# A small language-model tower in one kernel: another order of steps, sums and norms in its mixer

## The chip, the cores and the metric

The kernel runs as one program on one core of a Trainium2 chip. The metric is the device time of one execution in microseconds (us); lower is better. A core has a matrix engine (TensorE, PE in the profile), three engines for element-wise work (VectorE = DVE, ScalarE = ACT, GpSimd = POOL) and SyncE (SP), which issues most DMAs. Each engine works through its own queue in order, and semaphores tie the queues together.

## The reference

16 sequences of 128 tokens (2048 rows of width 192, 16 tiles of 128 rows) go through an embedding with a LayerNorm, an attention block, a mixer and a mixture of experts, all in float32:

```python
h = _L0_tok_ref(ids, types, token_emb, pos_emb, type_emb, gamma, beta)
h = h + attn(layernorm(h))                 # 8 heads of 192, softmax, projection
h = h + ffn(layernorm(h))                  # the function below

def ffn(x):
    h = _ln(x, ln1_g, ln1_b)               # a second norm of the normed rows
    q, k, v = split(h @ in_w.T + in_b)     # 12 heads of 16
    attn = softmax(q @ k.T / 4)            # over the 128 tokens of a sequence
    x = x + (attn @ v) @ out_w.T + out_b
    x = x + gelu(x @ mlp_w1 + mlp_b1) @ mlp_w2 + mlp_b2
    xm = _ln(x, ln2_g, ln2_b)
    return x + sum over the top 2 of 4 experts of gate * (gelu(xm @ w1 + b1) @ w2 + b2)
```

The mixer of the kernel is the part of `ffn` up to and with the line with `out_w`. Its input x is a normed row, so it needs two norms of each row, the norm and the norm of the norm.

## The kernel before, in words

Four stages follow each other, with all engines meeting in between: `embed`, `attention` (8 turns of 2 tiles), `mixer` (line 750, 16 tiles in 4 units of 4), and `experts`.

In attention each engine walks the same text of steps (`TURN`, line 353); words with a + are work for the next turn and are left out of the last. Ahead of the last turn SyncE asks for 14 finished tiles of h1 for the mixer (line 485).

In the mixer a list `order` (lines 799 to 828) names steps, and each engine walks it (`walk_order`), doing its own part of each step. The steps are: N, norms of a unit, in 15 parts, on VectorE; X, 8 transposes of the normed rows and their split into a high and a low half (ScalarE, then VectorE); Q0 to Q2, projections of q and k, of five passes each; V0 to V3, of v; S, the scores of a tile (12 heads in 4 strips of 3) and their row maxima on VectorE; M, the exponentials on ScalarE, 12 of 128x128; T, 12 transposes of them on TensorE, copied out strip by strip by ScalarE; A, the mix with v and, with a matrix of ones, the sums of the probabilities (lines 986, 990), which VectorE inverts as 128x384 numbers and multiplies in (lines 1138, 1141) to make the context; O, the projection out (line 999), which VectorE adds to the rows (line 1147) and SyncE stores.

For tile t the order is S(t), T(t-1), M(t), A(t-1), parts of the next unit's X, Q, V and N, O(t-1). TensorE writes X, Q, V, T, A and O into four banks in turn (`ring`); a slot waits until the slot four before it has been emptied (`emptied`, line 858). The scores have four banks of their own and are written when the exponentials before them have been read.

Beside this GpSimd prepares the weights of the experts: for each of 5 it loads them, splits off the high halves with three one-operand instructions (lines 908 to 910) and makes the low halves with three two-operand ones (lines 911 to 913). In the mixer the short helper lines 123 to 144 are those of moments and inverse roots.

## Time and profile before

| what | value |
|---|---|
| time, median of 3 runs | 1055.23 us (1053.48 to 1067.02) |
| the profiled execution's own time | 1057.01 us |
| its span, first to last instruction | 1055.3 us |
| TensorE busy | 824.1 us (78%) |
| VectorE, ScalarE, GpSimd busy | 545.9, 466.9, 229.9 us |

The page cuts the span into 40 slices of 26.4 us; a digit is the busy share in tenths, PEclk the granted clock of TensorE in tenths of full speed. The mixer lies in slices 18 to 27 (of 1 to 40).

```profile
PE   0039999999999999953365658655499999999997
DVE  5944242424334342327967775441456655765664
...
POOL 6221120202020111216761000000241250260260
PEclk9999999999999999985688988786699999999999
```

In a timeline row the first number is the start in us from the span's beginning, the second the length; then come engine, line, operation, what is written and read, and how many instructions are merged. In square brackets stands how long the engine was idle before, and what released it.

### The profile page before, as it was taken

The page shows a single profiled execution, that of the slowest core. Times are in us where ns is not written, and L with a number is a line of the kernel's source. Part 1 is how long each engine was busy: PE and PEld are TensorE (multiplying, and loading weights), DVE is VectorE, ACT ScalarE, POOL GpSimd, SP SyncE. Part 2 cuts the span into 40 slices and gives each one's busy share as a digit, 9 for nine tenths or more (in the row PEclk, how much of TensorE's full clock was granted, in tenths as well). Part 3 has the DMA queues.
Part 4 walks back from the last instruction along what each step waited for, and adds up shares of the span by engine and source line. Part 5 has one row for each costly group of instructions (what it writes and reads, how often), then busy time and mean ns, then how long its engine had stood idle before and what let it go on. Part 6 is the DMA issues. An engine that isn't in the chain of part 4 may idle for free. (4 is left out here: it accounts for less than half of the span.)

```text
span 1055.3 us, 17628 instructions
## 1 busy us (share of the span) xinstructions
PE 824.1 (78%) x5912; PEld 721.3 (68%) x5912; DVE 545.9 (52%) x1283; ACT 466.9 (44%) x1106; POOL 229.9 (22%) x311
## 2 busy tenths in 40 slices
PE   0039999999999999953365658655499999999997
PEld 0038989898989888842244446545389789788786
DVE  5944242424334342327967775441456655765664
ACT  2305444445353534411253534433065565465553
POOL 6221120202020111216761000000241250260260
PEclk9999999999999999985688988786699999999999
DMA  7133241423323232533220000002100010100000
GB/s 206 61 126 83 47 125 47 108 60 82 82 60 82 60 93 52 168 63 99 77 89 9 8 8 9 12 8 66 35 1 2 17 33 0 48 2 0 16 1 16
DMA packets 48889, 56.95 MB, mean 54 GB/s; under 512 B 7440, under 2 KB 43920, under 8 KB 48848
## 3 DMA queue, kind: packets, MB, share of 16 engines
q1 hardware_dynamic: 41232, 43.02, 15.1%
q0 software_dynamic: 2544, 9.05, 2.9%
q10 hardware_dynamic: 5072, 4.36, 1.9%
q8 instruction: 23, 0.38, 0.2%
q14 instruction: 18, 0.15, 0.0%
HBM read 37.54 MB, written 18.87 MB: 53 GB/s over the span
## 5 line engine op out<-in xcount | busy, mean ns | idle before, releaser
L1503 DVE TENSOR_TENSOR ffn_hid_lo<-ffn_gelu,ffn_hid_hi 128x512 fp32r<-128x512 f32 x120 | 95.7, 800 | 116.3 <-ACT ffn_hid_hi L1481 106.7
L1442 PE MATMUL ffn_ps_out<-ffn_weights_w,ffn_hid_hi 128*128 128x384 f32 x480 | 146.4, 361 | 3.1 <-DVE ffn_hid_lo L1503 1.9
L1478 ACT ACTIVATE ffn_gelu<-ffn_ring,ffn_b 128x512 f32<-128x512 f32 x120 | 82.2, 685 | 125.7 <-PE ffn_ring L1431 122.7
L1443 PE MATMUL ffn_ps_out<-ffn_weights_w,ffn_hid_lo 128*128 128x192 f32 x480 | 121.2, 252 | 0.0
L506 POOL TENSOR_SCALAR attn_probs<-attn_probs,attn_inverse 128x128 f32<-128x128 f32 x128 | 47.7, 373 | 332.1 <-DVE attn_inverse L729 324.4
L1442 PEld LDWEIGHTS ffn_ps_out<-ffn_weights_w,ffn_hid_hi 128*128 128x128 f32 x480 | 90.2, 188 | 13.5 <-DVE ffn_total L1561 4.1
L1443 PEld LDWEIGHTS ffn_ps_out<-ffn_weights_w,ffn_hid_lo 128*128 128x128 f32 x480 | 91.4, 190 | 4.3
L653 ACT ACTIVATE attn_probs<-ps_scores,attn_neg_max 128x128 f32<-128x128 f32 x128 | 45.2, 365 | 81.5 <-DVE attn_neg_max L725 81.5
L1481 ACT ACTIVATE ffn_hid_hi<-ffn_gelu 128x512 fp32r<-128x512 f32 x120 | 75.9, 632 | 3.8
L1046 ACT ACTIVATE mix_pt<-mix_ring 128x384 f32<-128x384 f32 x64 | 27.3, 494 | 82.2 <-PE mix_ring L973 81.2
L525 PE MATMUL ring<-ident,attn_xn 128*128 128x128 f32 x32 | 5.7, 305 | 69.5 <-DVE attn_xn L694 69.4
L736 DVE COPY attn_mixed_rows<-ps_pairs 128x256 f32<-128x256 f32 x32 | 13.6, 425 | 88.4 <-PE ps_pairs L588 50.9
L1040 ACT ACTIVATE mix_probs<-mix_ps_scores,mix_neg_max 128x128 f32<-128x128 f32 x192 | 51.4, 420 | 16.7 <-DVE mix_neg_max L1131 16.6
L999 PE MATMUL mix_ring<-mix_w_out,mix_context 128*128 128x192 f32 x96 | 27.9, 446 | 35.1 <-DVE mix_context L1141 35.1
L1138 DVE RECIPROCAL mix_inverse<-mix_ring 128x384 f32<-128x384 f32 x16 | 40.9, 2557 | 27.0 <-PE mix_ring L990 26.9
L525 PEld LDWEIGHTS ring<-ident,attn_xn 128*128 128x128 f32 x32 | 3.6, 150 | 72.3 <-DVE attn_xn L694 72.3
L1377 POOL TENSOR_SCALAR ffn_bias_part<-ffn_b,ffn_gates 128x192 f32<-128x192 f32 x64 | 32.7, 527 | 91.3 <-DVE ffn_gates L1540 88.8
L999 PEld LDWEIGHTS mix_ring<-mix_w_out,mix_context 128*128 128x128 f32 x96 | 22.7, 264 | 41.6 <-DVE mix_context L1141 41.1
L603 PE MATMUL ps_scores<-w_proj_main,attn_mixed_rows 128*128 128x192 f32 x256 | 49.1, 326 | 0.8 <-ACT attn_mixed_rows L667 0.7
L644 ACT ACTIVATE attn_q_main<-ring,attn_b_qk 128x256 f32<-128x256 f32 x64 | 30.4, 475 | 37.2 <-PE ring L537 33.7
L721 DVE TENSOR_TENSOR attn_v_flat<-ring,attn_b_v 128x512 f32<-128x512 f32 x48 | 33.1, 690 | 26.3 <-PE ring L549 25.0
L667 ACT ACTIVATE attn_mixed_rows<-ps_mixed 128x512 f32<-128x512 f32 x32 | 19.2, 599 | 60.5 <-PE ps_scores L603 34.1
(291 smaller groups left out, 2299.7 us busy)
## 6 DMA issues: line engine op xcount, KB each, us to landing
v_rows<-attn_v_flat SPq DMA_DIRECT2D x16, 768.0 KB, 3.2
attn_v_rows<-v_rows SPq DMA_DIRECT2D x128, 96.0 KB, 3.3
mix_stage<-in_w POOLq DMA_DIRECT2D x5, 576.0 KB, 5.8
embed_stage_main<-in_w_qkv SPq DMA_DIRECT2D x3, 768.0 KB, 5.6
mix_stage<-in_w POOLq DMA_DIRECT2D x10, 192.0 KB, 3.2
mix_stage<-in_w POOLq DMA_DIRECT2D x5, 384.0 KB, 4.0
attn_xin<-h_rows ACTq DMA_DIRECT2D x8, 192.0 KB, 4.4
last_emb<-h_rows SPq DMA_DIRECT2D x8, 192.0 KB, 2.5
```

The lines of the kernel that those rows point to most:

```text
L506: last = nc.gpsimd.tensor_scalar(probs[:, n, j, :], probs[:, n, j, :], inverse[:, n, j:j + 1], float(D) ** -0.5, ALU.mult, ALU.mult)
L603: last = nc.tensor.matmul(out_of(b), mixed_rows[:, c, :], w, start=c == 0, stop=c == KTILES - 1)
L653: last = nc.scalar.activation(probs[:, n, j, :], ps_scores[:, n % 2, j, :], ACT.Exp, bias=neg_max[:, n, j:j + 1], accum_out=sums[:, n, j:j ...
L721: nc.vector.tensor_tensor(v_flat[:, cols], ring[:, bank(slot), :], b_v[:, cols], ALU.add).then_inc(emptied["dve"].sem, 1)
L999: last = nc.tensor.matmul(ring[:, bank("O", t), 0:D], context[:, s, :], w_out[:, s, :], start=s == 0, stop=s == SETS - 1)
L1040: last = nc.scalar.activation(probs[:, i, s, :], ps_scores[:, i, s * P:(s + 1) * P], ACT.Exp, bias=neg_max[:, i, s:s + 1])
L1138: steps.then(nc.vector.reciprocal(inverse[:, :, :], by_set(1)))
L1442: nc.tensor.matmul(ps_out[:, b, 0:2 * D], hid_hi[:, i % 3, tile], w2[:, c, :, :], start=c == 0, stop=False)
L1443: last = nc.tensor.matmul(ps_out[:, b, 0:D], hid_lo[:, i % 3, tile], w2[:, c, 0, :], start=False, stop=c == HC - 1)
L1478: nc.scalar.activation(gelu[:, i % 2, :], ring[:, bank(slot), :], ACT.Gelu, bias=b1[:, f * HC + c:f * HC + c + 1]).then_inc(chunk_read.sem, 1)
L1481: nc.scalar.activation(hid_hi[:, i % 3, :], gelu[:, i % 2, :], ACT.Copy).then_inc(hi_ready.sem, 1)
L1503: nc.vector.tensor_tensor(hid_lo[:, i % 3, :], gelu[:, i % 2, :], raw(hid_hi[:, i % 3, :]), ALU.subtract).then_inc(lo_ready.sem, 1)
```

## The change

Five things are changed together.

1. The sums of the probabilities come from the exponentials (`accum_out`), 12 numbers a row. VectorE inverts those 12 in a step I; 12 matmuls against the identity spread them over the rows of the context's layout, ScalarE copies that, and the matmuls with ones and the large reciprocal go.
2. Norms of units 0 to 2, and the mixer's input of unit 0, are steps Z of VectorE in attention's last turn (words with a -). The last unit's norms (L) lie in the mixer's tiles 1 and 2.
3. For tile t the order is now T(t-1), I(t-1), S(t), A(t-1), the parts of the next unit, W, L, O(t-1); exponentials belong to S. The maxima are taken strip by strip.
4. GpSimd makes only the high halves of the experts' weights; the low halves are steps W of VectorE, 15 in all. GpSimd's loads of an expert wait for the halves of the one before.
5. Two of the four copies of step Q2 move from ScalarE to VectorE.

```diff
+TWICE_PARTS = 2 * ROOT_PARTS + 2
...
+def twice_normed(nc, steps, norm, part, tiles):
...
+    half, guess, work, spread, second = (t[:, tiles] for t in norm["scratch"])
+    moments, rstd, both = norm["moments"], norm["rstd"][:, tiles], norm["both"][:, tiles]
+    if part < ROOT_PARTS:
+        inverse_root(nc, steps, part, moments[:, tiles, 1], 1e-5, half, guess, rstd, work)
+    elif part == ROOT_PARTS:
+        steps.then(nc.vector.tensor_tensor(spread, rstd, rstd, ALU.mult))
+        steps.then(nc.vector.tensor_tensor(spread, spread, moments[:, tiles, 1], ALU.mult))
+    elif part < TWICE_PARTS - 1:
+        inverse_root(nc, steps, part - ROOT_PARTS - 1, spread, 1e-5, half, guess, second, work)
+    else:
+        steps.then(nc.vector.tensor_tensor(both, rstd, second, ALU.mult))
...
+def mixer_input(nc, steps, norm, hin, part, unit):
...
+    zn, wide = norm["zn"], lambda row: row[:, :].unsqueeze(1).to_broadcast([P, MIX_UNIT, D])
+    if part == 0:
+        for i in range(MIX_UNIT):
+            t = unit * MIX_UNIT + i
+            last = nc.vector.tensor_scalar(zn[:, i, 0:D], hin[:, t, :], norm["moments"][:, t, 0:1], norm["both"][:, t:t + 1], ALU.subtract, ALU.mult)
+        steps.then(last)
+    elif part == 1:
+        steps.then(nc.vector.tensor_tensor(zn[:, :, 0:D], zn[:, :, 0:D], wide(norm["gain"]), ALU.mult))
+    else:
+        steps.then(nc.vector.tensor_tensor(zn[:, :, 0:D], zn[:, :, 0:D], wide(norm["shift"]), ALU.add))
+        nc.vector.tensor_copy(zn[:, :, D:D + TAIL], zn[:, :, MAIN:D]).then_inc(norm["zn_ready"], 1)
@@ attention, the last turn @@
+        TURN = """S0 +N0 +N1 S1 +N2 I0 V3 +N3 +N4 V4 +N5 I1 S2 V5 +X0 S3 T0 +Q0 I2 I3 +Q1 T1 +Q2 M0 R0 -Z0 +Q3 +Q4 +Q5 M1 R1
+                  -Z1 -Z2 +Q6 +Q7 T2 +Q8 +Q9 O0 +Q10 O1 T3 -Z3 -Z4 +Q11 O2 M2 R2 -Z5 -Z6 -Z7 +V0 O3 +Q12 F0 -Z8 -Z9 +Q13 M3 R3
+                  -Z10 -Z11 -Z12 -Z13 -Z14 +V1 +Q14 +Q15 +V2 +Q16 O4 +Q17 +Q18 O5 +Q19 +Q20 +Q21 +Q22 +Q23 O6 O7 -Z15 F1"""
...
             act.wait_ge(biases_loaded, 48)
+            for row, name in (("gain", "ln1_g"), ("shift", "ln1_b")):
+                act.dma_start(keep["norm"][row][:, :], dram[name].to_broadcast([P, D])).then_inc(keep["ln1_loaded"], 16)
@@ attention, VectorE @@
+            def mixer_norm(turn, part, slot, hi, source):
...
+                norm = keep["norm"]
+                if part < 3:
+                    if part == 0:
+                        dve.wait_ge(keep["hin_loaded"], 16)
+                    tiles = range(part * MIX_UNIT, (part + 1) * MIX_UNIT)
+                    moments_of(nc, mix_steps, norm["stats"], norm["moments"][:, tiles.start:tiles.stop, :], [keep["hin"][:, t, :] for t in tiles])
+                elif part < 3 + TWICE_PARTS:
+                    twice_normed(nc, mix_steps, norm, part - 3, slice(0, 3 * MIX_UNIT))
+                else:
+                    if part == 3 + TWICE_PARTS:
+                        dve.wait_ge(keep["ln1_loaded"], 32)
+                    mixer_input(nc, mix_steps, norm, keep["hin"], part - 3 - TWICE_PARTS, 0)
+
             def finish(turn, b, slot, hi, source):
@@ mixer, the order @@
+        LAST_NORM = 1 + TWICE_PARTS
+        projections(0, "X Q0 Q1 Q2")
         for t in range(TILES + 1):
             unit, j = divmod(t, UNIT)
+            if t:
+                order.extend((("T", t - 1), ("I", t - 1)))
             if t < TILES:
                 order.append(("S", t))
             if t:
-                order.append(("T", t - 1))
-            if t < TILES:
-                order.append(("M", t))
+                order.append(("A", t - 1))
             if t == 0:
-                norms(1, range(NORM_PARTS))
-            elif unit + 1 < UNITS and j == 0:
-                norms(unit + 1, range(10, NORM_PARTS))
-            if t:
-                order.append(("A", t - 1))
+                projections(0, "V0 V1 V2 V3")
             if unit + 1 < UNITS:
-                projections(unit + 1, {0: "", 1: "X Q0", 2: "Q1 Q2", 3: "V0 V1 V2 V3"}[j])
-            if unit + 2 < UNITS and j > 1:
-                norms(unit + 2, {2: range(0, 5), 3: range(5, 10)}[j])
+                inputs(unit + 1, {0: (0, 1, 2), 3: (3,)}.get(j, ()))
+                projections(unit + 1, {0: "", 1: "X Q0", 2: "Q1 Q2 V0", 3: "V1 V2 V3"}[j])
+            if t == 0:
+                inputs(0, (3,))
+            if 0 < t < TILES:
+                order.append(("W", t - 1))
+            if t in (1, 2):
+                half_way = LAST_NORM // 2
+                order.extend(("L", part) for part in (range(half_way) if t == 1 else range(half_way, LAST_NORM)))
             if t:
                 order.append(("O", t - 1))
@@ mixer, GpSimd @@
...
-                w2_hi, w2_lo = w2[:, :, 0, :], w2[:, :, 1, :]
+                w1_hi, _, _, w2 = keep["ffn"][f]
+                if f:
+                    pool.wait_ge(weights_lo, 3 * f)
                 for half_rows in range(2):
...
-                main, tail = stage[:, 0, :], stage[:, 1, :]
-                nc.gpsimd.tensor_scalar(w1_hi[:, :], main, 1.0, 1.0, ALU.mult, ALU.mult)
-                nc.gpsimd.tensor_scalar(w2_hi, stage2[:, :, :], 1.0, 1.0, ALU.mult, ALU.mult)
-                steps.then(nc.gpsimd.tensor_scalar(w1_half[:, :], tail, keep["low_rows"][:, 0:1], 1.0, ALU.mult, ALU.mult))
-                nc.gpsimd.tensor_tensor(w1_lo[:, :], main, raw(w1_hi[:, :]), ALU.subtract)
-                nc.gpsimd.tensor_tensor(w2_lo, stage2[:, :, :], raw(w2_hi), ALU.subtract)
-                steps.then(nc.gpsimd.tensor_tensor(w1_stack[:, :], tail, raw(w1_half[:, :]), ALU.subtract))
+                nc.gpsimd.tensor_scalar(w1_hi[:, :], stage[:, 0, :], 1.0, 1.0, ALU.mult, ALU.mult).then_inc(weights_hi, 1)
+                nc.gpsimd.tensor_scalar(w1_half[:, :], stage[:, 1, :], keep["low_rows"][:, 0:1], 1.0, ALU.mult, ALU.mult).then_inc(weights_hi, 1)
+                nc.gpsimd.tensor_scalar(w2[:, :, 0, :], stage2[:, :, :], 1.0, 1.0, ALU.mult, ALU.mult).then_inc(weights_hi, 1)
@@ mixer, TensorE @@
+            def spread_inverse(t):
+
+                pe.wait_ge(inverse_ready, t + 1)
+                slot_free("I", t)
+                for s in range(SETS):
+                    for i in range(STRIPS):
+                        wide = inverse[:, i, s:s + 1].to_broadcast([P, PAIR])
+                        last = nc.tensor.matmul(ring[32 * i:32 * i + 32, bank("I", t), s * P:(s + 1) * P], wide, keep["ident"][:, :], start=True, stop=True)
+                last.then_inc(spread, 1)
...
                         rows = slice(32 * i, 32 * i + 32)
-                        nc.tensor.matmul(ring[rows, bank("A", t, 0), s * P:(s + 1) * P], v_pad[:, unit % 2, b, i * SETS + s, :], pt[:, i, s, :], start=True, stop=True)
-                slot_free("A", t, 1)
-                for i in range(STRIPS):
-                    rows = slice(32 * i, 32 * i + 32)
-                    last = nc.tensor.matmul(ring[rows, bank("A", t, 1), 0:WIDE], ones[:, :], pt[:, i, :, :].rearrange("p s k -> p (s k)"), start=True, stop=True)
@@ mixer, ScalarE @@
-                            last = nc.scalar.activation(probs[:, i, s, :], ps_scores[:, i, s * P:(s + 1) * P], ACT.Exp, bias=neg_max[:, i, s:s + 1])
-                    last.then_inc(exps_ready, 1)
+                for i in range(STRIPS):
+                    act.wait_ge(max_ready, STRIPS * t + i + 1)
+                    for s in range(SETS):
+                        last = nc.scalar.activation(probs[:, i, s, :], ps_scores[:, i, s * P:(s + 1) * P], ACT.Exp, bias=neg_max[:, i, s:s + 1], accum_out=sums[:, i, s:s + 1])
+                    if i % 2:
+                        last.then_inc(exps_ready, 1)
+
+            def take_inverse(t):
+                act.wait_ge(spread, t + 1)
+                nc.scalar.activation(inverse_rows[:, :, :], ring[:, bank("I", t), 0:WIDE].rearrange("p (s k) -> p s k", k=P), ACT.Copy).then_inc(rows_ready, 1)
 
@@ mixer, VectorE @@
+            def split_weights(i):
+
+                f, part = divmod(i, 3)
+                w1_hi, w1_lo, w1_stack, w2 = keep["ffn"][f]
+                dve.wait_ge(weights_hi, 3 * f + part + 1)
+                to, of, hi = ((w1_lo[:, :], stage[:, 0, :], w1_hi[:, :]), (w1_stack[:, :], stage[:, 1, :], w1_half[:, :]),
+                              (w2[:, :, 1, :], stage2[:, :, :], w2[:, :, 0, :]))[part]
+                nc.vector.tensor_tensor(to, of, raw(hi), ALU.subtract).then_inc(weights_lo, 1)
...
+                    nc.vector.tensor_scalar(k_main[:, unit % 2, :, 0, :], by_tile, b_qk[:, 1:2], even[:, 0:1], ALU.add, ALU.mult)
+                    nc.vector.tensor_scalar(k_main[:, unit % 2, :, 1, :], by_tile, b_qk[:, 1:2], odd[:, 0:1], ALU.add, ALU.mult).then_inc(main_ready, 1)
+                    return
+                for rows in (slice(0, TAIL), slice(TAIL, P)):
+                    last = nc.vector.tensor_scalar(q_tail[rows, unit % 2, :], of[0:TAIL, :], b_qk[0:TAIL, 2:3], float(HD) ** -0.5, ALU.add, ALU.mult)
+                last.then_inc(q_tail_ready, 1)
...
+                for i in range(STRIPS):
+                    dve.wait_ge(scored, STRIPS * t + i + 1)
+                    nc.vector.tensor_reduce(out=neg_max[:, i, :], in_=ps_scores[:, i, 0:WIDE].rearrange("p (s k) -> p s k", k=P),
                                             op=ALU.max, axis=X, negate=True).then_inc(max_ready, 1)
...
+            def invert(t):
+                dve.wait_ge(exps_ready, 2 * t + 2)
+                nc.vector.reciprocal(inverse[:, :, :], sums[:, :, :]).then_inc(inverse_ready, 1)
...
-                steps.then(nc.vector.reciprocal(inverse[:, :, :], by_set(1)))
+                dve.wait_ge(rows_ready, t + 1)
                 if t:
                     dve.wait_ge(out_filled, t)
-                nc.vector.tensor_tensor(context[:, :, :], by_set(0), inverse[:, :, :], ALU.mult).then_inc(context_ready, 1)
+                nc.vector.tensor_tensor(context[:, :, :], by_set, inverse_rows[:, :, :], ALU.mult).then_inc(context_ready, 1)
```

## Rows read from the trace of the kernel before

**Rows 1.** busy time of each engine in the mixer's stretch: us, then busy (instructions), clock

```profile
467.60:714.50 246.90, 135.75 (x1228) 104.91 (x1228) 162.08 (x314) 95.80 (x284) 60.74 (x54) 0.79 0.13 39
```

**Rows 2.** costliest groups of the page: busy, mean ns | idle before, releaser

```profile
L1138 DVE RECIPROCAL mix_inverse<-mix_ring 128x384 f32<-128x384 f32 x16 | 40.9, 2557 | 27.0 <-PE mix_ring L990 26.9
...
L1046 ACT ACTIVATE mix_pt<-mix_ring 128x384 f32<-128x384 f32 x64 | 27.3, 494 | 82.2 <-PE mix_ring L973 81.2
...
L999 PEld LDWEIGHTS mix_ring<-mix_w_out,mix_context 128*128 128x128 f32 x96 | 22.7, 264 | 41.6 <-DVE mix_context L1141 41.1
```

**Rows 3.** timeline of one plain tile: start us, length us, engine, line, operation

```profile
680.86 1.24 PE L960 MATMUL mix_ps_scores<-mix_k_main,mix_q_main 32*128 32x256 f32 x8
...
682.55 1.82 DVE L1131 TENSOR_REDUCE mix_neg_max<-mix_ps_scores 128x6 f32<-128x768 f32 x2 [1.23 <-PE mix_ps_scores L963]
...
685.14 3.21 ACT L1040 ACTIVATE mix_probs<-mix_ps_scores,mix_neg_max 128x128 f32<-128x128 f32 x12
...
685.32 0.86 PE L986 MATMUL mix_ring<-mix_pt,mix_v_pad 128*32 128x128 f32 x24 [0.69 <-ACT mix_pt L1046]
...
690.10 1.78 PE L999 MATMUL mix_ring<-mix_w_out,mix_context 128*128 128x192 f32 x6 [3.27 <-DVE mix_context L1141]
...
691.82 1.24 PE L960 MATMUL mix_ps_scores<-mix_k_main,mix_q_main 32*128 32x256 f32 x8
```

**Rows 4.** timeline of the mixer's start

```profile
470.73 1.14 DVE L140 BATCH_NORM_STATS2 mix_stats<-hin 128x6 f32<-128x192 f32 x4
...
477.92 1.25 DVE L1091 TENSOR_SCALAR mix_zn<-hin,mix_moments,mix_both 128x192 f32<-128x192 f32 x4
...
482.73 7.20 DVE L1102 TENSOR_SCALAR hin<-hin,mix_moments,mix_rstd 128x192 f32<-128x192 f32 x4
...
482.87 1.97 PE L927 MATMUL mix_ring<-ident,mix_zn 128*128 128x128 f32 x8 [17.93 <-DVE mix_zn L1099]
...
492.31 0.80 PE L938 MATMUL mix_ring<-mix_zt_hi,w_mix_hi 128*128 128x512 f32 x1 [7.47 <-DVE mix_zt_lo L1109]
...
501.55 0.71 PE L960 MATMUL mix_ps_scores<-mix_k_main,mix_q_main 32*128 32x256 f32 x8
```

**Rows 5.** DMA view, 430 to 720 us: issues, KB each, us to landing

```profile
hin<-h_rows SPq DMA_DIRECT2D x1, 1344.0 KB, 7.4
```

**Rows 6.** timeline of VectorE at attention's end

```profile
457.48 0.43 DVE L736 COPY attn_mixed_rows<-ps_pairs 128x256 f32<-128x256 f32 x1 [6.57 <-PE ps_scores L603]
...
460.12 0.42 DVE L736 COPY attn_mixed_rows<-ps_pairs 128x256 f32<-128x256 f32 x1 [1.36 <-PE ps_pairs L588]
...
465.08 0.36 DVE L745 TENSOR_TENSOR last_emb<-ps_scores,last_emb 128x192 f32<-128x192 f32 x1 [4.53 <-PE ps_scores L603]
```

**Rows 7.** groups of VectorE in the mixer, by form

```profile
L1117 DVE TENSOR_SCALAR mix_k_main<-mix_ring,mix_b_qk,mix_even 128x512 f32<-128x512 f32 x4 | 3.2, 803 | 4.4 <-PE mix_ring L938 4.4
...
L1096 DVE TENSOR_TENSOR mix_zn<-mix_zn,mix_gain 128x768 f32<-128x768 f32 x4 | 3.8, 958 | 0.1
```

**Rows 8.** timeline of maxima and exponentials in attention's last unit

```profile
433.14 0.69 DVE L725 TENSOR_REDUCE attn_neg_max<-ps_scores 128x4 f32<-128x512 f32 x1 [1.52 <-PE ps_scores L562]
...
433.86 0.37 ACT L653 ACTIVATE attn_probs<-ps_scores,attn_neg_max 128x128 f32<-128x128 f32 x1 [4.19 <-DVE attn_neg_max L725]
...
434.22 0.36 ACT L653 ACTIVATE attn_probs<-ps_scores,attn_neg_max 128x128 f32<-128x128 f32 x1
```

**Rows 9.** timeline of TensorE in a denser tile of the mixer

```profile
584.49 1.14 PE L999 MATMUL mix_ring<-mix_w_out,mix_context 128*128 128x192 f32 x6
...
586.42 1.53 PE L973 MATMUL mix_ring<-ident,mix_probs 128*128 128x128 f32 x12
```

**Rows 10.** timeline of GpSimd: a load of weights and the first split

```profile
490.11 1.10 POOL L903 DMA_DIRECT2D mix_stage<-in_w  x2 [0.29 <-POOL ffn_weights_w_stack L913]
...
497.13 0.83 POOL L908 TENSOR_SCALAR ffn_weights_w_hi<-mix_stage 128x768 fp32r<-128x768 f32 x1 [4.51 <-DMA mix_stage<-in_w]
```

**Rows 11.** timeline, the mixer's last instruction on VectorE

```profile
712.05 0.36 DVE L1147 TENSOR_TENSOR mix_x<-mix_ring,hin 128x192 f32<-128x192 f32 x1 [1.70 <-PE mix_ring L999]
```

180 lines of the change are left out of this document (74 added, 106 removed).

## The prediction

> **What bounds the kernel now.** I read the page's slices first, then the busy times of the stage where they dip, then the costliest groups, then one tile in order of time. Attention and the experts keep TensorE at 9 or near it in most slices. The mixer, 246.9 us from 467.6 to 714.5, has it busy for 136 us, at a granted clock of 0.79 [rows 1]. So the mixer is latency, not throughput. The groups name it: a reciprocal of 128x384 that takes 2.56 us, sixteen times, and ScalarE idle for over 80 us ahead of its copies of the turned probabilities [rows 2].
>
> The tile shows the loop [rows 3]. TensorE waits for the context, projects out (O), does the next scores (S), and only then turns the probabilities of the tile before (T), though they were ready long ago; ScalarE copies them, TensorE mixes (A), VectorE inverts 384 columns and multiplies, O again. S to S is 10.96 us (680.86 to 691.82), and the 3.2 us of exponentials lie hidden behind the mix and the reciprocal. Nothing but this ring of waits ends last. The other loss is the way in: VectorE norms unit 0 from 470.73, TensorE gets its first transposes at 482.87, then waits until 492.31 because the split behind them stands in VectorE's queue behind four row scalings that take 7.2 us; the first scores start at 501.55 [rows 4]. The same form of instruction took 1.25 us for four at 477.92: the long ones lie beside GpSimd's splits.
>
> **The change, part by part.** Times are against the profiled execution, 1057.0 us with a span of 1055.3; the median of the runs is 1055.2, so what I get is some 1.8 us high by the median.
>
> *Norms in attention's last unit.* 16 steps (Z) are put into VectorE's queue. Z0 waits for 14 tiles of h1, whose load takes 7.4 us to land [rows 5]; it is issued ahead of the unit, and Z0 stands behind that unit's first mix: no wait. Moments cost some 1.6 us a unit, the whole chain of moments and both roots 7.2 us (470.73 to 477.92) [rows 4]; 12 columns instead of 4 change nothing in such small instructions. Most lies in VectorE's idle time. Not all: after the third copy of the tails (released at 457.48) come Z5 to Z7 (8 small steps, 0.2 each: 1.6), the two adds of the first tile (0.9 to 1.0), Z8 and Z9 (7 steps, 1.4), and only then the last copy, now at 460.12 [rows 6]: 457.9 + 3.9 = 461.8. The second tile's projection hangs from it and ends 1.6 later. Z10 to Z15 (0.2 x 7, and the input of unit 0: 1.25 + 1.0 + 1.3) need 4.9 from 462.2 to 467.1, where VectorE waits 4.53 now [rows 6], so the last add comes at 467.1 instead of 465.08: +2.0 us. Two more DMA issues on ScalarE's queue at attention's start (0.5 us each) lie before its first work; nothing.
>
> *Way in.* The block starts at 469.6 instead of 467.6. TensorE transposes at once (2.0 us). ScalarE issues four small DMAs instead of six and splits from 471.5; VectorE's setup waits for a 2.5 us bias load and splits by 474.1. From the first projection to the first scores it was 9.24 us (492.31 to 501.55) [rows 4]; V0 to V3 move behind S0 and two of ScalarE's four copies go to VectorE (0.80 each by its nearest form [rows 7]), so 7.5 us. S0 at 481.6: 20 us earlier.
>
> *A plain tile.* New order T I S A O. From the start of S, at TensorE's high level (2.4 GHz): maxima start 1.69 behind S at the low one (680.86 to 682.55 [rows 3]), so I take half, 0.85, for the first strip. A reduction of 128x384 isn't in the trace; between 0.36 (128x192 forms) and 0.69 (128x512 [rows 8]), I take 0.56. The exponentials then run 4 x 3, each with a sum. In attention, with such sums, one starts 0.36 after the other [rows 8] against 3.2/12 = 0.27 here [rows 3]: 4.3 us, so they end at 5.75, and this now stands on the chain. Behind them: the last two strips turned (half of 1.53 [rows 9]), the inverse of 12 columns beside it (0.2), spreading it by 12 small matmuls. Those aren't in the trace. Their nearest row is the mix, the same 24 passes of the same size: 0.86 us with its tail [rows 3], 0.7 to the next start, which I take. Below, it could cost nothing if the copies still hold the chain; above stands a full 128-column load in every pass (0.264 [rows 2] x 24 = 6.3). Next S at 7.3 instead of 10.96. ScalarE's copies (four of 0.49 and one more) end at 7.9, before the next maxima; VectorE has 2.0 + 0.6 + 1.0 to 1.4 (weight half) + 0.4 + 0.2 of 7.3: hidden.
>
> *Tiles with projections or norms.* There VectorE's queue decides, for the inverse stands behind all of it, and the fourth turned strip waits for the bank that O's add frees. Again from the start of S; in each VectorE has done maxima and context by 3.5:
> - second of a unit: ScalarE splits only when its exponentials end, at 5.75; it and VectorE (0.7 a half) are through at 7.6; Q0's five passes 1.4, O 1.1 [rows 9], T 1.4, I 0.7: 12.2.
> - third: four copies of 0.80 [rows 7], with overlap 3.0, v 0.4, a weight half 0.96 [rows 7] (1.4 for 1152 columns), the add 0.36: 8.2; fourth strip 0.4, I 0.7: 9.3.
> - fourth: row scalings 1.25 + 1.0, three v's of 0.36, half, add: 8.1; then as before, 9.2.
> - first: the input steps 1.25 + 1.0 + 1.3, half, add: 8.4; 9.5.
>
> The last unit's norms (7.2 us) go into tiles 1 and 2 instead of being spread: 14.2 and 12.4. S0 to S1, with V0 to V3, the input steps and the row scalings ahead of the inverse, 12.
>
> *Weight halves.* GpSimd loads expert f+1 only when VectorE has finished the 3 halves of f. From issue to its first split is 7.0 us (490.11 to 497.13), 0.8 more to that split's end [rows 10]. Gaps between halves 3f+2 and 3f+3 are 8.6, 8.2, 10.3 and, in the tail, 5.9: one stall of about 2 us, 0.7 left on the chain (8.0 instead of 7.3).
>
> *Sum.* S to S from tile 0: 12, 14.2, 12.4, 9.2 | 9.5, 12.2, 9.3, 9.2 | 9.5, 12.2, 9.3, 9.2 | 7.3, 8.0, 7.3, and 10.3 from S15 to the last add: 161.1. The clock: the mixer has 0.79 now [rows 1], with TensorE idle for 3.27 us ahead of each plain O [rows 3]; 0.79 is the low level (1.2 GHz) for 42% of the time. Per plain tile 2.3 us of TensorE's work lie on the new chain, so 1.0 us a tile, 16 in all, if that stays. Gaps get shorter in plain tiles (1.7 us), longer ones remain in the second tiles and at the start, so I take 5, and 3 for handovers that my chain leaves out. S0 to end: 169, against 210.9 (501.55 to 712.4) [rows 4, 11]. End at 481.6 + 169 = 650.6 instead of 712.4: 61.8 us less, and the experts' stage is not touched. 1057.0 - 61.8 = 995.
>
> **The rivals.**
> - *VectorE and GpSimd block each other.* The 7.2 us beside GpSimd's two-operand splits [rows 4] show it. GpSimd keeps its 15 one-operand splits, 0.83 us for 768 columns [rows 10], a third of them of 1152: 14.5 us in all. VectorE takes the 15 others, with two operands from memory. For: both now work in tiles where VectorE's queue decides. Against: GpSimd's slow half is gone. At worst all 14.5 us come on: 1010. The Trainium skill (SBUF — State Buffer, Practical consequences) says that a VectorE instruction with two SBUF inputs contends with a GpSimd one that reads SBUF, and one instruction waits for the whole of the other; by that rule the weight halves are the ones to suffer. The long row scalings agree with the lock as such.
> - *The clock stays low.* If denser work doesn't raise it, all PE terms double: 2.3 x 16 = 37 instead of 5, end 1027; at 0.79, 1006. Against: in a denser tile, around 585, O takes 1.14 where the plain tile has 1.78 [rows 3, 9].
> - *Spreading costs what a full load costs.* If each of the 24 passes of I waits for its weights at 0.264 us [rows 2], I takes 6.3 us instead of 0.7, on the chain of all 16 tiles: +90 us, 1085, slower by 2.6%. It decides from 0.24 us a pass: 5.8 a tile, +82, past 1078. For: its operand is one column read 32 times, a form of which there is no row. Against: mixes of the same count take 0.86.
> - *Hidden anyway.* If VectorE's queue holds every tile of the first three units to 13 us and the tail at 9, S0 to end is 12 x 13 + 4 x 9 + 3 = 195: 1021. The stage can't easily be worse than before, as 2.4 us of reciprocal a tile are gone from a chain on which they stood.
>
> **How the numbers follow.** Forecast, 985 to 1005: 0.55. Better (maxima, handovers and clock all at the good end: 8 us of slack not needed, and first tiles quicker): 0.10. Locks or low clock, 1005 to 1022: 0.22. Queue case and both together, 1022 to 1034: 0.05. Spreading dear: 0.06, half of it within 2%, half slower; anything else within 2%, 0.02. A comparison of this kernel tells 2% (21 us) from no change: faster below 1034, 0.92; same 0.05; slower 0.03. The range runs from 979 (all bounds good) to 1019.
>
> **What would show it.** Right: first scores near 481 to 482; attention's last add near 467; plain tiles S to S of 7 to 8 us, led by exponentials 0.36 apart; in tiles with projections TensorE waiting for VectorE; experts starting near 652 with their stage still 341 us. Wrong: I longer than 1.5 us; weight halves well over 1.4 us; granted clock in the mixer under 0.8; a tail pitch over 9 us.

## The result and the profile after

The changed kernel takes 1004.75 us (median of 4 runs, 1003.39 to 1005.92) against 1056.7 us of the kernel before on the same chip: ratio 0.949, 95% interval 0.942 to 0.956. The profiled run took 1005.92 us with a span of 1004.2 us. The forecast was 995, range 979 to 1019.

The slices of the page (TensorE, VectorE, GpSimd, granted clock; 25.1 us each) show the mixer at slices 19 to 27 of 40:

```profile
PE   0029999999999999986667758645999999999997
DVE  4954242424242425236576555524357566566564
POOL 7320101111111111021102012201061160260260
PEclk9999999999999999999688989978799999999999
```

TensorE is still not full there. The busy times of the mixer's stretch (us; then PE, PEld, DVE, ACT, POOL, each with its instructions; granted clock; DMA share; GB/s):

```profile
474.10:663.20 189.10, 128.71 (x1484) 103.98 (x1484) 108.65 (x251) 116.32 (x484) 30.57 (x40) 0.87 0.17 50
```

It was 246.9 us at a clock of 0.79 [rows 1]. So 57.8 us went here, and 6.5 came back ahead of it: attention's last add is at 471.59, not 465.08 [rows 6]. The experts take 341.0 us, and 340.8 before.

The way in, in order of time (start, us, engine, line, operation, [idle before, releaser]):

```profile
474.13 1.06 PE L977 MATMUL mix_ring<-ident,norm_zn 128*128 128x128 f32 x8 [2.67 <-PEq L349]
478.70 0.79 PE L988 MATMUL mix_ring<-mix_zt_hi,w_mix_hi 128*128 128x512 f32 x1 [3.50 <-DVE mix_zt_lo L1161]
486.27 1.24 PE L1011 MATMUL mix_ps_scores<-mix_k_main,mix_q_main 32*128 32x256 f32 x8 [1.96 <-DVE mix_q_tail L1175]
```

The first scores start 14.7 us behind attention's last add, where it took 36.5 before [rows 4, 6].

A plain tile, the answer to [rows 3]:

```profile
642.79 0.71 PE L1011 MATMUL mix_ps_scores<-mix_k_main,mix_q_main 32*128 32x256 f32 x8
643.65 0.86 PE L1046 MATMUL mix_ring<-mix_pt,mix_v_pad 128*32 128x128 f32 x24
643.74 1.95 DVE L1190 TENSOR_REDUCE mix_neg_max<-mix_ps_scores 128x3 f32<-128x384 f32 x4 [2.14 <-PE mix_ps_scores L1014]
644.33 0.37 ACT L1091 ACTIVATE mix_probs<-mix_ps_scores,mix_neg_max 128x128 f32<-128x128 f32 x1 [0.92 <-DVE mix_neg_max L1190]
644.69 0.36 ACT L1091 ACTIVATE mix_probs<-mix_ps_scores,mix_neg_max 128x128 f32<-128x128 f32 x1
...
646.21 1.24 PE L1055 MATMUL mix_ring<-mix_w_out,mix_context 128*128 128x192 f32 x6 [1.70 <-DVE mix_context L1203]
647.29 0.82 PE L1023 MATMUL mix_ring<-ident,mix_probs 128*128 128x128 f32 x6
...
648.46 1.70 ACT L1102 ACTIVATE mix_pt<-mix_ring 128x384 f32<-128x384 f32 x4
```

The maxima start 0.95 us behind the scores and the exponentials run 0.345 apart. Behind them stands half of the turning, with the reciprocal (0.22) beside it, then the spread (0.86). The next scores start at 650.29: 7.50 us instead of 10.96. From the first scores to the last add it is 174.6 us, against 210.9. The scores start at 486.27 and then 13.95, 15.2, 12.4, 10.0 | 11.3, 14.55, 9.5, 11.3 | 9.7, 14.0, 9.4, 8.9 | 7.5, 8.9, 7.5 us apart, with 10.6 to the end.

### The profile page after: what moved, and what is told of

Its sections match the earlier page's. It is cut to its first block and busy times, and to the rows that moved or that the text cites. A ratio compares the mean times of both kernels' runs of the same rounds, so it can differ in the third digit from the quotient of the medians.

```text
span 1004.2 us, 18328 instructions
## 1 busy us (share of the span) xinstructions
PE 818.1 (81%) x6168; PEld 721.8 (72%) x6168; DVE 504.3 (50%) x1280; ACT 487.8 (49%) x1306; POOL 200.3 (20%) x295
## 5 line engine op out<-in xcount | busy, mean ns | idle before, releaser
L1504 PEld LDWEIGHTS ffn_ps_out<-ffn_weights_w,ffn_hid_hi 128*128 128x128 f32 x480 | 90.2, 188 | 13.5 <-DVE ffn_total L1623 4.1
L1091 ACT ACTIVATE mix_probs<-mix_ps_scores,mix_neg_max 128x128 f32<-128x128 f32 x192 | 67.4, 391 | 19.0 <-DVE mix_neg_max L1190 19.0
L1190 DVE TENSOR_REDUCE mix_neg_max<-mix_ps_scores 128x3 f32<-128x384 f32 x64 | 31.2, 551 | 40.3 <-PE mix_ps_scores L1014 40.3
L1023 PE MATMUL mix_ring<-ident,mix_probs 128*128 128x128 f32 x192 | 28.3, 285 | 22.3 <-DVE mix_x L1209 11.1
L642 PEld LDWEIGHTS ps_scores<-w_proj_main,attn_mixed_rows 128*128 128x128 f32 x256 | 42.5, 196 | 2.6 <-issue 2.2
L1091 ACT ACTIVATION_READ_ACCUMULATOR mix_probs<-mix_ps_scores,mix_neg_max 128x1 f32 x192 | 44.3, 231 | 0.0
```

Of the source, the lines that this page charges most:

```text
L642: last = nc.tensor.matmul(out_of(b), mixed_rows[:, c, :], w, start=c == 0, stop=c == KTILES - 1)
L1091: last = nc.scalar.activation(probs[:, i, s, :], ps_scores[:, i, s * P:(s + 1) * P], ACT.Exp, bias=neg_max[:, i, s:s + 1], accum_out=sums[ ...
L1504: nc.tensor.matmul(ps_out[:, b, 0:2 * D], hid_hi[:, i % 3, tile], w2[:, c, :, :], start=c == 0, stop=False)
```

## The experiments

What each profile shows, in us ("attention's turn" is the mean of the six turns ahead of the last, from last add to last add, "last turn" goes from there to attention's last add; "to the last add" is from the mixer's first scores to the end of its last add; ratios are to the kernel before on the same chip):

| run | median | ratio | span | attention's turn | last turn | first scores | to the last add | plain tile |
|---|---|---|---|---|---|---|---|---|
| before | 1056.7 | 1 | 1055.3 | 48.45 | 33.8 | 501.55 | 210.9 | 10.96 |
| changed | 1004.75 | 0.949 | 1004.2 | 49.27 | 36.9 | 486.27 | 174.6 | 7.50 |
| u_pool | 1018.4 | 0.959 | 1014.7 | 49.21 | 37.0 | 485.75 | 186.3 | 7.50 |
| u_order | 1013.6 | 0.955 | 1008.3 | 49.20 | 37.9 | 486.83 | 177.9 | 8.75 |
| u_sums | 1026.9 | 0.965 | 1026.4 | 49.29 | 37.0 | 487.57 | 195.2 | 10.17 |
| u_norms | 1022.9 | 0.961 | 1020.1 | 49.42 | 33.8 | 504.59 | 172.1 | 7.50 |
| i_twice | 1017.3 | 0.954 | 1016.5 | 49.33 | 38.2 | 488.34 | 184.9 | 8.16 |
| no_sums | 1004.4 | 0.943 | 1004.0 | 49.24 | 38.0 | 488.02 | 173.1 | 6.69 |
| b_pad | 1066.6 | 1.002 | 1066.7 | 49.51 | 33.8 | 508.29 | 214.8 | 10.96 |
| a_pad | 1003.2 | 0.942 | 1001.9 | 49.17 | 36.9 | 485.34 | 173.8 | 7.49 |
| z_early | 1001.5 | 0.940 | 997.4 | 49.21 | 35.1 | 483.32 | 170.4 | 7.49 |
| before_again | 1063.95 | - | 1062.2 | 48.29 | 35.2 | 500.93 | 217.4 | 10.94 |
| v1 | 983.4 | 0.924 | 978.9 | 49.22 | 36.1 | 484.80 | 151.2 | 7.49 |
| v2_pad96 | 976.7 | 0.916 | 974.4 | 48.41 | 33.8 | 477.18 | 153.4 | 7.49 |

The kernel before took 1063.5 to 1066.0 us (medians) on the later chips, so medians compare within a chip and by ratio; the parts are compared by their own stretches.

How much two profiles differ by themselves can be read off the table. before_again is the program of before, and takes 6.5 us more to the last add, at a granted clock of 0.79 there instead of 0.83. The changed kernel, u_norms, a_pad and z_early have the same steps behind the first scores and take 170.4 to 174.6 us, at 0.86 to 0.91. So a few us in that column are not shown by one profile. The ratios have such a spread too: a_pad is the changed kernel with 32 bytes left empty, its turns are as long, and it has 0.942 (0.938 to 0.946) on its chip where the changed kernel has 0.949 (0.942 to 0.956) on its own.

**u_pool, the weights' low halves back on GpSimd** (whose loads then no longer wait for VectorE).

```
- order.append(("W", t - 1))                  # VectorE: to = of - hi
+ nc.gpsimd.tensor_tensor(w1_lo, stage_main, w1_hi, ALU.subtract)   # and two more
```

> The changed kernel with one part undone: the low halves of the experts' weights are made on GpSimd again, by three two-operand instructions an expert, and nothing of it is left in VectorE's queue. Theory (VectorE's queue decides in the tiles with projections or norms, and GpSimd's slow halves disturb it little): 15 halves of 0.95 to 1.35 us leave that queue, 9 to 12 of them in deciding tiles, and the stall on the last experts' halves goes: 5 to 12 us faster than 1004.8, 993 to 1000. Rival (the part paid because it ended a block between the two engines): VectorE's row scalings grow from 0.375 us to the 1.07 us of before, other SBUF instructions with them, 11 us or more come on: 1012 to 1018. The row scalings' mean and the mixer's stretch (189 us now) tell them apart. Attention's turns: 49.0 to 49.6 us as in the changed kernel if its slower loads come from the changed layout of memory, 48.3 to 49.0 if they came from that one run.

The rival is right. The tail's stall is gone (7.5 three times), but the early tiles take 15.97, 14.3, 17.2, 17.3, 16.5: +11.7 us from first scores to last add, +10.5 in the span. VectorE's groups in the mixer (busy, mean ns, idle before), then the same groups of the changed kernel:

```profile
L181 DVE TENSOR_SCALAR norm_zn<-hin,norm_moments,norm_both 128x192 f32<-128x192 f32 x12 | 12.4, 1096 | 0.0
L1146 DVE TENSOR_SCALAR hin<-hin,norm_moments,norm_rstd 128x192 f32<-128x192 f32 x16 | 9.8, 672 | 0.0
```

```profile
L181 DVE TENSOR_SCALAR norm_zn<-hin,norm_moments,norm_both 128x192 f32<-128x192 f32 x12 | 3.7, 376 | 0.0
L1145 DVE TENSOR_SCALAR hin<-hin,norm_moments,norm_rstd 128x192 f32<-128x192 f32 x16 | 5.0, 375 | 0.0
```

The mechanism can be read off one place of u_pool, VectorE and then GpSimd:

```profile
522.56 1.22 DVE L164 TENSOR_TENSOR norm_spread<-norm_rstd 128x4 f32<-128x4 f32 x1
523.81 2.54 DVE L165 TENSOR_TENSOR norm_spread<-norm_spread,norm_moments 128x4 f32<-128x4 f32 x1
526.39 1.73 DVE L123 TENSOR_SCALAR norm_work<-norm_spread 128x4 f32<-128x4 f32 x1
528.15 0.17 DVE L124 TENSOR_SCALAR norm_half<-norm_work 128x4 f32<-128x4 f32 x1
```

```profile
521.96 1.80 POOL L961 TENSOR_TENSOR ffn_weights_w_lo<-mix_stage,ffn_weights_w_hi 128x768 fp32r<-128x768 f32 x1
523.72 2.62 POOL L962 TENSOR_TENSOR ffn_weights_w<-mix_stage,ffn_weights_w 128x1152 fp32r<-128x1152 f32 x1
526.29 1.80 POOL L963 TENSOR_TENSOR ffn_weights_w_stack<-mix_stage,mix_w_half 128x768 fp32r<-128x768 f32 x1
```

Four columns take 2.54 us: each of the three VectorE instructions ends as GpSimd's does (523.8, 526.3, 528.1). The reductions of the scores, which stand in PSUM, keep their mean of 0.55 us. By the Trainium skill (SBUF — State Buffer, Who interferes with whom) one of the two waits for the whole of the other's instruction; these rows agree. My expectation took the freed VectorE time as the larger side, and it was the smaller: 11.7 us is what is left of the block after that time is taken off.

**u_order, the old order of steps.**

```
- T(t-1) I(t-1) S(t) A(t-1)          # S: scores, maxima and exponentials
+ S(t) T(t-1) I(t-1) M(t) A(t-1)     # M: exponentials
```

> The changed kernel with the order of steps of before (scores of the next tile ahead of the turned probabilities, spread inverse behind them, exponentials after that); sums, norms and weights as changed. Theory: the loop now runs scores 1.1, maxima to 2.8, reciprocal 0.2, spread 0.8, its copy 0.5, exponentials 4.5: 8.8 us a plain tile instead of 7.5, the same 1.3 us in the others: +20 us, 1025. Rival A (VectorE's queue holds 12 of 16 tiles whatever the order): only the four tail tiles lose, +5 us, 1010. Rival B (the order was the main part of the gain, because the old one also puts the mix and the projection on the chain as before): 10.5 us a plain tile, +45 us, 1050.

A plain tile takes 8.75 us, as the theory's 8.8. The others don't lose, as rival A has it: the sum to the last add is only 3.3 us longer, the span 4.1. That is no more than the spread above, the profiled execution was the fastest of its four (1010.1, median 1013.6), and the ratio's interval (0.948 to 0.961) overlaps with that of the changed kernel. So of the four parts the order is the smallest, and beyond the plain tiles its price isn't shown.

**u_sums, the sums by ones and a reciprocal of 128x384.**

```
- nc.scalar.activation(probs, scores, ACT.Exp, bias=neg_max, accum_out=sums)
- reciprocal of 128x12, then 24 passes that spread it
+ matmul(ring, ones, pt)             # 8 passes of 32x384
+ nc.vector.reciprocal(inverse_rows, ring)    # 128x384
```

> The changed kernel with the sums as before: a mix with a block of ones gives them spread, VectorE inverts 128x384 in 2.56 us, the exponentials make no sums; order, norms and weights as changed. Theory: the reciprocal stands in VectorE's queue, which decides in the tiles with projections or norms (+2.3 us each, 12 tiles), and holds the output projection in plain tiles, 8.5 instead of 7.5 us: +31 us in all, 1036. Rival (with the new order the reciprocal hides behind the exponentials, which without sums start 0.27 instead of 0.39 us apart, and the spread leaves the chain): a plain tile takes 6 us, and the kernel takes 990 to 1000, so that the new order alone made the gain.

+20.5 us to the last add, +22.2 in the span: the theory's side, two thirds of its size. The plain tile is worse than expected, 10.17:

```profile
658.22 2.55 DVE L1205 RECIPROCAL mix_inverse_rows<-mix_ring 128x384 f32<-128x384 f32 x1
...
661.41 1.66 PE L1060 MATMUL mix_ring<-mix_w_out,mix_context 128*128 128x192 f32 x6 [3.64 <-DVE mix_context L1208]
662.87 2.77 PE L1024 MATMUL mix_ring<-ident,mix_probs 128*128 128x128 f32 x12
```

The reciprocal delays the projection, TensorE idles 3.64 us, and the 12 transposes then take 2.77 us at a granted clock of 0.52, the low level (1.47 at the high one). So the new order with the old sums is hardly faster in a plain tile than the kernel before (10.17 against 10.96).

**u_norms, the norm steps at the mixer's start.**

```
- TURN: ... -Z0 ... -Z15             # in attention's last turn
+ order = [("Z", part) for part in range(16)] + order
```

> The changed kernel with the norms of 12 tiles and the input of the first unit made at the mixer's start, not in attention's last unit. Theory: moments 4.9, two roots 5.6 and the input 3.6 us come before the first transposes, 14.1 us, less the 3 us that attention's end gets back: first scores 10 to 12 us later, near 497, 1015 in all; last adds of attention 3 us earlier against its own turns. Rival (VectorE's steps cost attention's end as much as they save, because its TensorE falls to the low clock there): within 4 us of 1004.8. Attention's turns again: 49.0 to 49.6 us if the layout does it.

First scores 33.9 us behind attention's last add instead of 14.7; attention's last turn takes 33.8 us, as before, and so gives 3.1 back (of which only 1.4 to 1.9 are the steps', see z_early); 15.9 us in the span. That is more than expected, since the steps start only 5.8 us behind the last add (the setup waits for a bias) and meet GpSimd's splits, here one-operand ones (VectorE, then GpSimd):

```profile
485.21 0.74 DVE L128 TENSOR_TENSOR norm_work<-norm_second 128x12 f32<-128x12 f32 x1
485.98 0.86 DVE L129 TENSOR_TENSOR norm_work<-norm_work,norm_half 128x12 f32<-128x12 f32 x1
486.88 1.09 DVE L130 SCALAR_TENSOR_TENSOR norm_second<-norm_work,norm_second 128x12 f32<-128x12 f32 x1
```

```profile
485.11 0.83 POOL L961 TENSOR_SCALAR ffn_weights_w_hi<-mix_stage 128x768 fp32r<-128x768 f32 x1 [7.95 <-DMA mix_stage<-in_w]
485.93 0.90 POOL L962 TENSOR_SCALAR mix_w_half<-mix_stage,low_rows 128x768 fp32r<-128x768 f32 x1
486.80 1.14 POOL L963 TENSOR_SCALAR ffn_weights_w<-mix_stage 128x1152 fp32r<-128x1152 f32 x1
```

In spans the four parts undone cost 10.5, 4.1, 22.2 and 15.9 us, 52.7 in all, where the whole change brings 51.1. That the two are so near is no finding. By the medians the four are 62.8 us, on another chip, and by the ratios (0.9, 0.5, 1.5 and 1.2%) 4.2%, some 45 us, so whether the parts overlap stays open. The ranking is firmer: the four ran on one chip against the same runs of before, and spans, medians and ratios all give it. The change's fifth part, the two copies of Q2, was not undone by itself.

**i_twice, the 24 spreading passes run twice** (with 32 bytes left empty, so it compares with a_pad, below, on the same chip).

```
- for s in range(SETS): for i in range(STRIPS):
+ for s, i in [...] * 2:
```

> The changed kernel with each of the 24 passes that spread the inverse run twice (the second writes the same values again): the price of this step, by itself and on the chain. Theory (the spread stands on every tile's chain, 0.86 us for 24 passes at the high clock): +0.75 us a plain tile (7.5 to 8.25), and in the other tiles +0.75 to +1.5 us by the clock: +13 to +18 us. Rival (ScalarE's copies of the turned strips and VectorE's queue hold the tile, the spread is partly hidden): under +6 us.

Against a_pad a plain tile takes 8.16 instead of 7.49, and the way to the last add is 11.1 us longer, 0.69 a tile: a little below the theory's range. The medians on that chip, 1017.3 and 1003.2, differ by 14.1 us, which lies in it; 3 us of that come ahead of the first scores, where nothing was changed. The rival (under 6) is out. So 24 passes with one column read 32 times cost 0.67 us on the chain of a plain tile, 28 ns a pass. The doubled passes:

```profile
660.61 1.52 PE L1032 MATMUL mix_ring<-ident,mix_inverse 128*32 128x128 f32 x48
```

**no_sums, exponentials that make no sums** (so the softmax is not divided by its sums).

```
- ... ACT.Exp, bias=neg_max, accum_out=sums[:, i, s:s + 1])
+ ... ACT.Exp, bias=neg_max)         # sums: 128.0, filled in once
```

> The changed kernel with the exponentials making no sums; the inverse is that of a constant filled in at the start, so the softmax is not divided by its sums. All other steps stay. It prices the sums as such. Theory (the exponentials stand on the chain, 0.39 us apart with sums and 0.27 without): 1.4 us less a tile, 6.1 instead of 7.5 in plain ones, 16 to 22 us in all, if nothing else is late next. Rival (VectorE's queue or ScalarE's copies hold the tiles with projections and norms, so only four plain tiles gain): 5 to 8 us less.

12 exponentials take 3.2 us instead of 4.15, yet the plain tiles gain 0.8 and 0.25 and the one between them takes 10.13 instead of 8.91; to the last add 1.6 us less, within the spread, and in the span nothing. Both expectations miss. Behind the shorter exponentials the projection is next (in a plain tile it ends at 631.8, and they at 631.9), and the faster tiles only wait longer for the weights that GpSimd prepares. VectorE idles 3.21 us for them, its add comes late, and with it the bank for TensorE's last strip:

```profile
640.38 0.96 DVE L1157 TENSOR_TENSOR ffn_weights_w_lo<-mix_stage,ffn_weights_w_hi 128x768 fp32r<-128x768 f32 x1 [3.21 <-POOL ffn_weights_w_hi L960]
641.26 0.35 DVE L1210 TENSOR_TENSOR mix_x<-mix_ring,hin 128x192 f32<-128x192 f32 x1
641.66 0.90 PE L1023 MATMUL mix_ring<-ident,mix_probs 128*128 128x128 f32 x3 [2.21 <-DVE mix_x L1210]
```

**a_pad and b_pad, 32 bytes a partition left empty**, in the changed kernel and in that of before.

```
+ sb("pad", [P, 8])
```

> The changed kernel with 32 bytes a partition left empty behind the norms' tiles that it keeps through attention, and nothing else. Those tiles take 6304 bytes a partition, so attention's tiles that DMAs load (xin, v_rows) or store from (v_flat) begin 32 bytes off a multiple of 64 in the changed kernel and on one in the kernel before. Theory (the layout makes the loads slower, VectorE waits for xin, and TensorE for VectorE): with the 32 bytes attention's turns are 48.4 us again instead of 49.2 to 49.4, xin lands in 4.4 us instead of 5.0, and the kernel takes 5 us less, 1000 where the changed one takes 1005. Rival (it is something else of the change, such as the tables loaded at attention's start or the distance of the tiles): turns stay at 49.2 to 49.4.

> The kernel before with the same 32 bytes left empty, so that xin, v_rows and v_flat begin 32 bytes off a multiple of 64. Theory (layout): attention's turns go from 48.45 to 49.2 to 49.4 us, +5 to +6 us in all, which would be ratio 1.005. Rival: turns stay at 48.4 to 48.5, ratio 1.000.

They split: b_pad's turns are 49.51 us, a_pad's stay at 49.17. By these two the theory is half right, or the first profile of before was a lucky one. b_pad's ratio, 1.0016 (0.9988 to 1.0044), doesn't tell 1.000 from a small loss; the expected 1.005 lies just outside.

**before_again, the kernel before on a later chip.**

> The kernel before, unchanged, profiled on this chip. The 32 bytes moved nothing in the changed kernel, so what makes attention's turns 49.2 us and more in all later profiles is open. If the change does it, this profile has turns of 48.4 us and xin landing in 4.4 us, as the first one; if it is the run or the chip, 49.2 to 49.5 us and 4.9 or more.

48.29 us, and xin lands in 4.3: the change does it. What is left is the place. On multiples of 128 bytes turns are short, at 32 (b_pad, the changed kernel) or 64 off (a_pad) long. The granted clock is 1.00 in these turns in every profile, so it is not the clock. The test is v2_pad96, below.

**z_early, the norm steps at other places of the last turn** (with the 32 bytes).

```
- I2 I3 ... R0 -Z0 ... R1 -Z1 -Z2 ... T3 -Z3 -Z4 ... R2 -Z5 -Z6 -Z7 ... -Z15 F1
+ I2 -Z0 I3 ... -Z1 ... R0 -Z2 ... R1 -Z3 -Z4 -Z5 ... T3 -Z6 -Z7 ... R2 ... F1 -Z15
```

> The changed kernel with the 32 bytes left empty and the 16 norm steps at other places of attention's last turn: the moments while VectorE waits behind the second and third reciprocals, the first root before the third copy of the mixed tails, no step between that copy and the first add but those before the last copy, the last step behind the last add. Theory (the steps ahead of the copies delay TensorE's last projection, which then also runs at the low clock, 4.5 instead of 2.9 us): last add 33.8 us after the last turn's predecessor's, as before the change, instead of 36.9; first scores 3 us earlier relative to it; 3 us less than with the 32 bytes alone. Rival (steps only change places, and zn is ready later): first scores within 1 us of the 14.7 us behind the last add plus the delay that was, no gain.

Against a_pad the last turn takes 35.1 instead of 36.9, and first scores come 2.0 us earlier; ratio 0.940 against 0.942, which the timing alone can't tell apart. The last projection in the changed kernel, a_pad and z_early (before has z_early's, 2.87 us behind a gap of 0.70):

```profile
465.64 4.52 PE L642 MATMUL ps_scores<-w_proj_main,attn_mixed_rows 128*128 128x192 f32 x16 [2.13 <-issue]
```

```profile
465.68 2.84 PE L642 MATMUL ps_scores<-w_proj_main,attn_mixed_rows 128*128 128x192 f32 x16 [2.13 <-issue]
```

```profile
464.65 2.87 PE L642 MATMUL ps_scores<-w_proj_main,attn_mixed_rows 128*128 128x192 f32 x16 [0.70 <-ACT attn_mixed_rows L706]
```

The steps ahead of the copies lengthen TensorE's gap from 0.70 to 2.13 us, and z_early takes that away. The second half of my theory, that TensorE then comes back at the low clock, does not hold: only the changed kernel's profile shows it (4.52 us at 0.63), while u_pool, u_order, u_sums, i_twice, no_sums and a_pad have the same gap and then 2.84 us.

The last turn still isn't 33.8, and that is the clock at another place. Some 15 us into the last turn every profile has TensorE idle for 1.83 us ahead of a mix of eight passes; in some the clock then falls and in some it doesn't. The mix in before and in before_again, the same program:

```profile
445.99 1.13 PE L583 MATMUL ps_mixed<-attn_pt,attn_v_rows 128*128 128x128 f32 x8 [1.83 <-issue]
```

```profile
444.20 2.04 PE L583 MATMUL ps_mixed<-attn_pt,attn_v_rows 128*128 128x128 f32 x8 [1.84 <-issue]
```

Granted clock from 14 to 22 us into the last turn, and the last turn:

| steps ahead of the copies | clock 1.00 | 0.79 | 0.57 to 0.62 |
|---|---|---|---|
| none | before, b_pad, u_norms, v2_pad96: 33.8 | before_again, z_early: 35.1 | v1: 36.1 |
| as in the changed kernel | changed: 36.9 (with its 1.65 at the projection) | u_pool, u_sums, a_pad: 36.9 to 37.0 | u_order, i_twice, no_sums: 37.9 to 38.2 |

So the clock took 0, 1.3 or some 2.3 us there, by the run, and the place of the steps cost 1.85 us (a_pad against z_early, both at 0.79).

**v1, the steps placed by what was seen.**

```
+ X(next unit) ahead of S in second tiles, VectorE's split behind it
+ W(t-1) between I(t-1) and S(t), in place of behind A
+ N(unit, 3) in the unit's second tile; N(unit+2, 0 and 1) in the fourth
+ L over tiles 1 to 6; w1 of the next expert loaded after 2 of 3 halves
```

> A version built on the last one (early norm steps, 32 bytes empty), with the mixer's steps placed by what was seen: in a unit's second tile the next unit's transposes run ahead of the scores and ScalarE splits them while the maxima are made; VectorE does a weight half between the reciprocal and the maxima, where it waited; the row scalings move to their own unit's second tile, two of the three input steps to the tile before, the last unit's norms over tiles 1 to 6; GpSimd asks for the next expert's first weights when two of three halves are done; the setup of the masks stands behind the first split. Theory (in these tiles VectorE's queue and ScalarE's late split set the pitch, not the exponentials): second tiles fall from 14.0 to 11 us, first to second scores from 11.3 to 11, scores 1 to 3 from 28 to 22, plain tiles stay at 7.5 with no stall: 18 to 25 us less, 975 to 983. Rival (the tiles are held by the exponentials and the copies that follow them, and the split ahead only delays them): under 6 us less.

983.4 us, ratio 0.924 (0.918 to 0.930); to the last add 151.2, 19 us less than z_early, within the expected 18 to 25, and 18.5 less in the span. The tiles: 9.4, 10.45, 10.0, 11.4 | 9.3, 12.35, 9.4, 9.7 | 8.5, 10.7, 9.4, 7.5 | 7.5, 7.5, 7.5.

**v2_pad96, the same with 96 bytes empty.**

```
- sb("pad", [P, 8])
+ sb("pad", [P, 24])
```

> The last version with 96 bytes a partition left empty in place of 32, nothing else. Attention's turns so far: 48.3 to 48.45 us where xin, v_rows and v_flat begin on a multiple of 128 bytes (the kernel before, twice), 49.5 us where they begin 32 bytes off one (before with 32 empty), 49.2 to 49.4 us at 32 or 64 bytes off (the changed kernel and its variants). Theory (the loads want a multiple of 128 bytes): with 96 empty they begin on one again, turns are 48.4 us, xin lands in 4.4 us, and attention ends 5 us earlier: span 973 to 975 instead of 978.9, ratio to before about 0.919. Rival (not the place of these tiles, or a coarser one): turns stay at 49.2, ratio 0.9237.

Turns of 48.41 us, first scores 7.6 us earlier than in v1 (5.3 by the turns and what is ahead of them, 2.3 by the last turn's clock), 4.5 us less in the span, 976.7 us, ratio 0.916 (0.913 to 0.919; v1's interval begins at 0.918, and the two ran on different chips). The loads of xin (KB each, median us to landing) in before_again, b_pad, the changed kernel and v2_pad96:

```profile
attn_xin<-h_rows ACTq DMA_DIRECT2D x8, 192.0 KB, 4.3
```

```profile
attn_xin<-h_rows ACTq DMA_DIRECT2D x8, 192.0 KB, 5.6
```

```profile
attn_xin<-h_rows ACTq DMA_DIRECT2D x8, 192.0 KB, 5.0
```

```profile
attn_xin<-h_rows ACTq DMA_DIRECT2D x8, 192.0 KB, 4.2
```

VectorE's statistics wait for these loads 2.3 us in all in before's six turns ahead of the last, 8.6 in b_pad's, 6.8 in v1's and 2.0 in v2_pad96's.

The theory is confirmed in its effect. From before to b_pad the wait grows by 6.3 us and the six turns by 6.4; from v1 to v2_pad96 the wait falls by 4.8 and the turns by 4.9. So the wait for xin accounts for all of it, and v_rows, which also lands later (3.7 instead of 3.4), need not. In the fast cases the tiles begin on multiples of 256 bytes too, so the runs don't tell 128 from 256. The Trainium skill (DMA: Bandwidth & Descriptors, How a descriptor splits into AXI transactions) counts extra transactions for what does not start on a multiple of 256 bytes, and tells of the bytes fetched; here it is the place written that moves. The runs agree with that grain, but 32 bytes off (b_pad) is the slowest here, where its count would make it the cheapest of the three that are off (the others are 160 and 192), so the cause is open.

## Why the prediction was right, and where it fell short

The result lies in the range and just inside the likeliest case (985 to 1005), with 10 us (19% of the gain) fewer than forecast. The mixer's last add was to end at 650.6 and ends at 660.9: 4.5 us of that are there at attention's last add, 0.2 on the way in, 5.6 in the mixer. By its own steps:

- *A plain tile, 7.3*: 7.50. Every term stands in the rows: maxima 0.95 behind the scores (0.85), the first exponential 0.59 behind that (0.56), 4.15 for twelve (4.3), the spread 0.79 to the next scores (0.7). u_order and u_sums show that order and sums had to go together: with either undone the plain tile is back at 8.75 or 10.17.
- *Attention's end, +2.0*: right. By a_pad and z_early the steps cost 1.85 us. In the changed kernel's own profile it is 36.9 - 33.8 = 3.1, of which 1.4 is the longer gap and 1.65 the low clock at the projection, which six other profiles with the same gap don't have.
- *Way in*: from the last add to the first scores 14.7 us, as worked out (14.5). u_norms shows that the early norms carry 16 us of the gain.
- *Attention itself, "nothing"*: this is where the text was blind. Each of the turns became 0.8 us longer, 3.4 us net at the last turn's start, although no instruction of theirs changed. The kept norm tiles pushed attention's tiles off their places in memory, their loads land later, and VectorE's statistics wait for xin, 7.0 us in six turns instead of 2.3. b_pad and v2_pad96 show that the place does it.
- *Tiles with projections or norms*: the mixer is 13.5 us over the list, of which 8 were allowed for clock and handovers. The second tiles hold 5.2 of it (15.2, 14.55, 14.0 for 14.2, 12.2, 12.2), because the projection and O in them run at the low clock (0.53 from 558.0 to 561.5). The allowance for the clock was in the sum, so this is a size. The text put the last unit's norms, 7.2 us, at 2.0 and 3.1 in their tiles without saying why; the tiles took 15.2 and 12.4 for 14.2 and 12.4, so that held.

```profile
555.50 1.15 ACT L1070 ACTIVATE mix_zt_hi<-mix_ring 128x512 fp32r<-128x512 f32 x2
557.63 0.55 PE L988 MATMUL mix_ring<-mix_zt_hi,w_mix_hi 128*128 128x512 f32 x1 [4.90 <-DVE mix_zt_lo L1161]
559.68 1.94 PE L1055 MATMUL mix_ring<-mix_w_out,mix_context 128*128 128x192 f32 x6
561.46 1.47 PE L1023 MATMUL mix_ring<-ident,mix_probs 128*128 128x128 f32 x12
```

- *Weight halves, one stall in the tail*: three stalls, in the tiles with 11.3, 11.3 and 8.9 us, 4.8 us over the list where 0.7 was in it. From GpSimd's first issue to its first split are 8.1 to 8.5 us here, where the row of before had 7.0 [rows 10], and VectorE idles for it three times, 5.5 us in all:

```profile
L1156 DVE TENSOR_TENSOR ffn_weights_w_lo<-mix_stage,ffn_weights_w_hi 128x768 fp32r<-128x768 f32 x5 | 4.8, 955 | 5.5 <-POOL ffn_weights_w_hi L960 5.5
```

- *Rivals.* The block between VectorE and GpSimd did not come on VectorE's side: the halves take 0.955 and 1.348 us, the row scalings 0.375 [rows 4, 7]. It came on GpSimd's, off the chain: a split of 768 columns that meets a weight half takes 1.69 us (545.86) instead of 0.90. u_pool shows how dear the block is with two-operand splits on GpSimd, 11.7 us net. The text's sum took the short lengths for granted and did not name this as a gain. The clock stayed above 0.8 (0.87). Spreading is cheap, 0.86 us by the trace and 0.67 by i_twice.

Still open: what makes the clock fall behind the same gap in one run and not in another, and what in the loads the place of a tile changes.

## What to carry to other kernels

Take the chain apart before and after at the same place; a step is worth what it takes off the wait that ends last, and no_sums shows that a cheaper instruction there may give nothing once the next wait stands behind it. A VectorE instruction of four columns can take as long as the GpSimd instruction that it meets (2.54 and 2.62 us in u_pool), so look at what runs beside it before its size. Whoever keeps new tiles through an earlier stage should compare where that stage's DMA tiles now begin: the 96 empty bytes brought 4.9 us over six turns. And profile the kernel before a second time: here the same program differed by 1.3 us in the last turn and 6.5 in the mixer, more than some of the parts that one wants to price.
